# Layer 0 of a two-layer triangle-multiplication kernel: every projection unit as 64-row tiles, and two masks in four on VectorE

## The chip, the cores and the metric

The kernel runs on one NeuronCore of a Trainium2 chip. The metric is the device time of one launch, in microseconds. The kernel before has a median of 1039.27 us over three runs (1038.81 to 1039.66). The engines are named as in the profile: PE is TensorE (PEld its weight loads), DVE is VectorE, ACT is ScalarE, POOL is GpSimd, SP is SyncE, whose queue issues the DMAs.

## The reference, cut to what matters

The input is x[1, 256, 256, 64] in float32. There are two layers, each added to x after a group norm. Layer 0, the one that the change touches, is

```
zn = ln(gn(x))                                  # 256 x 256 tokens of 64 channels
a  = mask * sigmoid(zn @ w_ag + b_ag) * (zn @ w_ap + b_ap)
b  = mask * sigmoid(zn @ w_bg + b_bg) * (zn @ w_bp + b_bp)
p  = einsum('bikc,bjkc->bijc', a, b)
x  = x + (ln(p) @ w_z + b_z) * sigmoid(zn @ w_g + b_g)
```

Layer 1 is like it, without a mask, with whole-tensor norms in place of the layer norms, and with einsum('bitc,bjtc->bijc').

## The kernel before, in words

**Layout.** A row of 256 tokens is held as 128 partitions = 2 parities (q) x 64 channels, by 128 columns. Four rows are a group (64 groups), eight rows (PR) are a unit (NP = 32 units). The transposed, normalised x stays in SBUF as two float16 halves (hi and lo), and so do the weights. A product of x and w is hi*hi + hi*lo + lo*hi, so three matmuls.

**Chunks.** The 64 channels of a and b are made in NQ = 4 chunks of 16. For each chunk `chunk(q)` on the PE first projects the 32 units, and then does 16 einsum steps (one for each channel, four float32 matmuls of 256 columns in two halves). The two parts alternate: projections of chunk 0, einsum of chunk 0, projections of chunk 1, and so on. The PE projects units 2 to 31 of chunk q, then units 0 and 1 of the next chunk ahead, and then waits for all masks of the chunk (`msk_done`, `msk_done_v`) before the einsum.

**A unit in layer 0.** It passes four engines:

- PE, `project(q, n)`: 8 rows x 3 passes into the PSUM banks 2s and 2s+1, s = n % 4. The stationary operand is the x of one row (128 columns), the moving one the weights. What form the matmuls have is decided by `split_rows(layer, n)`, that is by SPLIT_ROWS. An even unit of layer 0 is split: two matmuls with 64 rows and 64 moving columns for each row and pass, one for each half of the array (`half_rows`), 48 in all. An odd unit is whole: one matmul with 128 rows and 128 moving columns, 24 in all. The halves of an even unit lie with their parities exchanged (`crossed(g)`), which the bank index `t ^ crossed(g)` undoes. A unit n of 4 or more waits for the product of unit n-4 (`prod_done`), which frees its banks.
- ACT, L971: one sigmoid of 128x512 from PSUM into the tile sig[u % 4]. It waits for the unit's matmuls and for the mask of the unit four before it, which reads the same tile (`masks_before`).
- DVE, L1397: the product of the linear part (PSUM) and the gate (SBUF), in place in sig.
- the mask, L377 (`mask_tile`): sig times the mask, both in SBUF, into ab. Of four masks the DVE does the one whose index u % 4 is in MASKS_V = (1,), and POOL does the other three. The DVE's own mask of unit u-1 stands in its queue right behind the product of unit u (`products(q, n8)`); POOL's waits for the product of its own unit.

**Order.** All orders are written by hand as each engine's instruction stream with semaphores. The DVE does the 32 products (with its masks among them), then for each of the 16 channels two additions of sums (L1416, L1419). ACT does the sigmoids, among them those of units 0 and 1 of the next chunk, and then two PSUM reads a channel (L1007, L1011). POOL has nothing but its masks in this stage. SP stores p in pairs of channels while the einsum runs. After chunk 3 the PE does the first four output gates (`project_gate`) in place of the next chunk's units.

**Layer 1** has units of both forms too (SPLIT_ROWS[1]), with two more matmuls a unit for a bias; units 2 and 3 of each eight are both split and follow one another. There the halves are never crossed.

Two lines show the widths that the form of a unit sets:

```
last = mm(PS[:, bank, r * QW:(r + 1) * QW], x[half_rows, :], w[half_rows, ...QW])   # split: QW = 64
last = mm(PS[:, 2 * s + r // GR, ...ROW], x, w[:, q * ROW:(q + 1) * ROW], ...)      # whole: ROW = 128
```

Of the kernel before, what the change touches and what calls it, by code (L numbers as in the profile page):

```python
# [76 lines left out]
E_Z = E_G + ROW  # L77
E_N = E_Z + ROW
UB = 8
SPLIT_ROWS = ((0, 2, 4, 6), (0, 2, 3, 5, 7))  # L80
EPS = 1e-5
Z_SCALE = 2.0 ** 8
W_TOP = 2.0 ** 13
# [13 lines left out]
def build(nc, x, mask, w0, w1, bias0, bias1, vecs, consts, norm_consts, spread, ones3, out):  # L97
# [16 lines left out]
    with ctx:  # L114
# [34 lines left out]
        def split_rows(layer, u):  # L149

            return u % UB in SPLIT_ROWS[layer]

# [184 lines left out]

        def crossed(g):

            return int(g // 2 % 2 in SPLIT_ROWS[0])  # L340

        assert all(split_rows(0, u) == crossed(2 * u) for u in range(UB))

        def group_rows(g):

# [7 lines left out]

            return tile.rearrange("p (b n) -> p b n", b=2)

        MASKS_V = (1,)
        MASKS_P = 4 - len(MASKS_V)

        def masks_before(n4, u):

            v = u % 4
            fours = n4 + u // 4
            if v in MASKS_V:
                return msk_done_v, fours * len(MASKS_V) + MASKS_V.index(v) + 1
            return msk_done, fours * MASKS_P + sum(w not in MASKS_V for w in range(v + 1))

# [155 lines left out]
        def _(pe):  # L522
# [98 lines left out]
            for step in range(max(NG + SUMS_LAG, spreads[-1][0] + 1)):  # L621
                if step < NG and step % 2 == 0:
                    n = step
                    reached(pe, sq_ready, n - 1)
                    for m in range(n, n + 2):
                        for q in range(2):
                            rows, to = (slice(h * CH, (h + 1) * CH) for h in (q, q ^ crossed(group_of(m))))
                            last = mm(cs_bank(m)[to, :], cs[rows, rows], group_rows(group_of(m))[rows, :])
                    last.then_inc(mm1_done, 2)
                n = step - SUMS_LAG  # L630
                if 0 <= n < NG:
                    square_sums(round_of[n], n - FIRST[round_of[n]])
                if step == 3:

                    small([(PS[:, 7, P:2 * P], ones, diag),
                           (PS[:, 7, 2 * P:2 * P + 1], out_sq, ones[:, 0:1])])
                for at_step, t, u in spreads:
                    if at_step == step:
                        spread_rstd(t, u)

            for layer in range(2):
# [19 lines left out]
                def project(q, n, bias=True):  # L661
# [12 lines left out]
                    for r in range(PR):  # L674
                        g, at_r = 2 * n + r // GR, r % GR
                        hi, lo = (half(g, i)[:, at_r * P:(at_r + 1) * P] for i in range(2))
                        for i, (x, w) in enumerate(((hi, w_hi), (hi, w_lo), (lo, w_hi))):
                            if split_rows(layer, n):
                                ends = r == 0 and i == 0, r == PR - 1 and i == 2
                                for t in range(2):  # L680
                                    half_rows = slice(t * CH, (t + 1) * CH)
                                    bank = 2 * s + (t ^ crossed(g) if layer == 0 else t)
                                    last = mm(PS[:, bank, r * QW:(r + 1) * QW], x[half_rows, :],
                                              w[half_rows, (2 * q + t) * QW:(2 * q + t + 1) * QW],
                                              ends[0] and not begun, ends[1] and (layer == 0 or begun))
                            else:
                                ends = at_r == 0 and i == 0, at_r == GR - 1 and i == 2
                                last = mm(PS[:, 2 * s + r // GR, at_r * ROW:(at_r + 1) * ROW], x,
                                          w[:, q * ROW:(q + 1) * ROW],
                                          ends[0] and not begun, ends[1] and (layer == 0 or begun))  # L690
# [39 lines left out]
                def chunk(q):  # L730
# [16 lines left out]
                    if layer == 0:  # L747
                        pe.wait_ge(msk_done, (q + 1) * (NP // 4 * MASKS_P))
                        pe.wait_ge(msk_done_v, (q + 1) * (NP // 4 * len(MASKS_V)))
                    else:  # L750
# [349 lines left out]
        def _(pool):  # L1100
# [13 lines left out]
            with pool.Fori(0, NQ) as q:  # L1114
                with pool.Fori(0, NP // 4) as n4:
                    for u in range(4):
                        if u not in MASKS_V:
                            pool.wait_ge(prod_done[0], q * NP + (n4 * 4 + (u + 1)))
# [557 lines left out]
```

## Time and profile before

| | |
|---|---|
| median of the runs | 1039.27 us (1038.81 to 1039.66) |
| the profiled execution | 1042.83 us, 3.56 us (0.34%) above that median |
| its span, first to last instruction | 1040.9 us |
| mean granted TensorE clock | 0.953 of full |
| busy over the span | PE 89%, DVE 73%, ACT 65%, POOL 46% |
| layer 0, projections of the four chunks | from 197, 266, 332 and 398 us |
| layer 0, einsums of the four chunks | from 236, 302, 367 and 433 us |

Times in the views are microseconds from the start of the span, unless marked ns. A row of a timeline merges instructions of one kind that follow each other, so that "x3" over 1.88 us is three of them, overlapping at their ends as their records do. The ends of matmuls are modelled; their starts are not, so the pace of the PE is read from counts in a stretch.

### The profile page before, as it was taken

What the parts mean: (1) busy time and instruction counts of PE and PEld (TensorE: products, weight loads), DVE (VectorE), ACT (ScalarE), POOL (GpSimd) and SP (SyncE); (2) the same over time, 40 slices, a digit from 0 to 9 for tenths busy, and PEclk for the clock granted to TensorE, in tenths of its full rate; (3) what the DMA queues carried; (4) which work ended last, traced back from release to release, by engine and by line L of the source; (5) the groups of instructions that cost most, each with busy time, mean ns of one, the idle gap of its engine ahead of it and who ended that gap; (6) DMA issues with size and microseconds to landing.
All of it is one profiled execution on the core that took longest, in us unless ns stands there. A gap on an engine that the chain in (4) does not pass through costs nothing.

```text
span 1040.9 us, 40845 instructions
## 1 busy us (share of the span) xinstructions
PE 927.0 (89%) x16740; PEld 743.7 (71%) x16740; DVE 763.9 (73%) x1276; ACT 673.4 (65%) x1104; POOL 476.6 (46%) x416
## 2 busy tenths in 40 slices
PE   5857877799999999978999996899999999869997
PEld 5732334698888988867898995678878788635554
DVE  5765898776868768688999998755646556458886
ACT  4659883566656666565777774575857758447775
POOL 0002667780752916506877882580936719200000
PEclk9879997799999999999999997899999999889999
DMA  9900000003113021179998940006032050389995
GB/s 333 377 23 2 2 2 2 3 4 121 45 43 122 4 106 60 49 215 261 223 217 192 219 91 1 3 4 163 4 89 78 7 160 4 89 200 294 359 325 192
DMA packets 159905, 122.06 MB, mean 117 GB/s; under 512 B 70788, under 2 KB 136708, under 8 KB 157704
## 3 DMA queue, kind: packets, MB, share of 16 engines
q1 hardware_dynamic: 159752, 119.74, 40.2%
q8 instruction: 131, 2.15, 0.9%
q14 instruction: 22, 0.18, 0.1%
HBM read 69.38 MB, written 50.33 MB: 115 GB/s over the span
## 4 chain that ended last, share of the span: by engine, by line
PE 74%; DVE 8%; ACT 6%; DMA 4%; issue 3%; POOL 2%; SPq 1%; DVEq 0%; POOLq 0%; ACTq 0%
PE PS L524 64%; PE PS L826 3%; DMA AB<-x 3%; PE PS L841 3%; ACT XT_ALL L931 2%; PE PS L873 2%; ACT AB L936 2%; PE PS L538 1%; POOL AB L377 1%; DVE AB L1359 1%; DMA AB<-k_scratch 1%; DVE XT_ALL L1361 1%; DVE XT_ALL L1529 1%; ACT WK L971 1%; SPq L391 1%
## 5 line engine op out<-in xcount | busy, mean ns | idle before, releaser
L524 PE MATMUL PS<-EFF,XT_ALL 64*128 64x64 f16 (+1 forms) x11112 | 326.3, 199 | 8.3 <-POOL XT_ALL L1105 3.2
L524 PEld LDWEIGHTS PS<-EFF,XT_ALL 64*128 64x128 f16 (+1 forms) x11112 | 296.6, 97 | 50.7 <-issue 25.8
L524 PE MATMUL PS<-AB 64*128 64x128 bf16 (+2 forms) x2058 | 239.9, 287 | 28.2 <-DVE XT_ALL L1361 13.0
L524 PEld LDWEIGHTS PS<-AB 64*128 64x128 bf16 (+2 forms) x2058 | 200.2, 123 | 68.5 <-issue 22.1
L971 ACT ACTIVATE WK<-PS,T 128x512 f32<-128x512 f32 x256 | 174.4, 685 | 94.8 <-PE PS L524 83.4
L1169 POOL TENSOR_TENSOR AB<-WK,AB 128x512 f32 x128 | 145.1, 1165 | 111.0 <-ACT AB L981 110.2
L377 POOL TENSOR_TENSOR AB<-WK,MS 128x512 f32 x96 | 130.6, 1390 | 105.5 <-DVE WK L1397 105.4
L1105 POOL TENSOR_TENSOR XT_ALL<-AB,XT_ALL 128x512 f16<-128x512 f32 x60 | 71.1, 1188 | 125.4 <-DVE XT_ALL L1361 120.4
L1405 DVE TENSOR_TENSOR WK<-PS,WK 128x512 f32<-128x512 f32 x128 | 85.8, 687 | 31.8 <-ACT WK L971 31.6
L1397 DVE TENSOR_TENSOR WK<-PS,WK 128x512 f32<-128x512 f32 x128 | 86.7, 689 | 30.2 <-ACT WK L971 25.0
L1421 DVE BATCH_NORM_STATS2 REC<-WK 128x512 f32 x64 | 44.5, 695 | 59.6 <-ACT WK L1000 59.6
L1000 ACT ACTIVATE WK<-PS,T 128x512 f32<-128x512 f32 x64 | 44.0, 688 | 54.4 <-PE PS L524 54.4
L1007 ACT ACTIVATE WK<-PS 128x512 f32<-128x512 f32 x64 | 41.1, 643 | 46.8 <-PE PS L524 46.8
L524 PEld LDWEIGHTS PS<-EFF,WK 128*128 128x128 f32 x512 | 68.5, 194 | 1.7
L524 PE MATMUL PS<-EFF,WK 128*128 128x128 f32 x512 | 68.0, 276 | 0.0
L1024 ACT ACTIVATE WK<-PS,T 128x512 f32<-128x512 f32 x64 | 46.4, 775 | 32.7 <-PE PS L524 32.7
L1416 DVE TENSOR_TENSOR S<-S,WK 128x512 f32<-128x512 f32 x64 | 44.6, 697 | 31.1 <-ACT WK L1007 30.3
L1067 ACT ACTIVATE WK<-PS 128x512 f32<-128x512 f32 x64 | 38.2, 597 | 44.2 <-PE PS L841 44.2
L1140 POOL TENSOR_TENSOR WK<-AB,S 128x256 f32<-128x256 f32 x64 | 50.5, 790 | 35.3 <-DVE S L1449 34.8
L981 ACT ACTIVATE AB<-WK 128x512 f32 (+1 forms) x96 | 60.0, 625 | 6.9 <-DVE WK L1405 6.9
L931 ACT ACTIVATE XT_ALL<-PS,T,CF 128x512 f32<-128x512 f32 x64 | 49.9, 780 | 18.1 <-PE PS L524 18.0
L1474 DVE SCALAR_TENSOR_TENSOR WK<-PS,T,WK 128x512 f32<-128x512 f32 x64 | 45.1, 746 | 21.8 <-PE PS L524 21.8
(199 smaller groups left out, 1435.5 us busy)
## 6 DMA issues: line engine op xcount, KB each, us to landing
AB<-x SPq DMA_DIRECT2D x64, 512.0 KB, 6.9
p_scratch<-WK SPq DMA_DIRECT2D x32, 512.0 KB, 2.6
k_scratch<-WK SPq DMA_DIRECT2D x128, 128.0 KB, 1.9
AB<-k_scratch SPq DMA_DIRECT2D x32, 512.0 KB, 11.1
out<-AB SPq DMA_DIRECT2D x16, 1024.0 KB, 7.6
AB<-p_scratch SPq DMA_DIRECT2D x29, 512.0 KB, 8.0
AB<-p_scratch SPq DMA_DIRECT2D x2, 640.0 KB, 5.7
AB<-spread SPq DMA_DIRECT2D x1, 896.0 KB, 7.4
```

The source lines that it names most:

```text
L377: return eng.tensor_tensor(ab[:, :, :, ds(n4 * (4 * PR) + u * PR, PR)], sig[:, u], rows.unsqueeze(2).to_broadcast([P, 2, 2 * CHUNK, PR]), ...
L524: return nc.tensor.matmul(dst, lhsT, rhs, start=start, stop=stop)
L931: nc.scalar.activation(group_rows(group_of(n)), cs_bank(n), ACT.Identity, bias=T[:, 15:16], scale=CF[:, C_NE0:C_NE0 + 1]).then_inc(zc_done, 1)
L971: nc.scalar.activation(tile, unit(layer, u)[:, :, 0:2 * CHUNK, :], ACT.Sigmoid, scale=T[:, 22:23] if layer == 0 else T[:, 28:29]).then_inc ...
L981: nc.scalar.activation(ab_rows(ab_hi, n8, u), sig1[:, u % UB], ACT.Copy).then_inc(abhi_done, 1)
L1024: nc.scalar.activation(gate1[:, k % 4], PS[:, k % 2, :], ACT.Sigmoid, bias=T[:, 32:33], scale=T[:, 28:29]).then_inc(gate1_ready, 1)
L1105: nc.gpsimd.tensor_tensor(lo, zn[:, n % 8], hi, ALU.subtract).then_inc(lo_done, 1)
L1140: nc.gpsimd.tensor_tensor(dst[:, 1], src[:, 1, :, u * GR:(u + 1) * GR, :], rs.to_broadcast([P, CH // 2, GR, 2]), ALU.mult).then_inc(pn_don ...
L1169: nc.gpsimd.tensor_tensor(ab_rows(ab_lo, n8, u), sig1[:, u], ab_rows(ab_hi, n8, u), ALU.subtract).then_inc(ablo_done, 1)
L1397: V.tensor_tensor(gate, lin, gate, ALU.mult).then_inc(prod_done[0], 1)
L1405: V.tensor_tensor(gate, lin, gate, ALU.mult).then_inc(prod_done[1], 1)
L1474: V.scalar_tensor_tensor(gate1[:, k % 4], PS[:, 4 + k % 2, :], col(34), gate1[:, k % 4], ALU.add, ALU.mult).then_inc(y1_done, 1)
```

## The change

SPLIT_ROWS[0] names all eight units, so the odd units of layer 0 take the split form as well; `crossed` keeps its values (1 for the groups of even units, 0 for those of odd ones), now written without SPLIT_ROWS. MASKS_V becomes (0, 2): the DVE multiplies the masks of the even units, each right behind the product of the odd unit that follows, and POOL those of the odd ones. The waits, `masks_before` and the counts MASKS_P follow from MASKS_V.

```
-SPLIT_ROWS = ((0, 2, 4, 6), (0, 2, 3, 5, 7))
+SPLIT_ROWS = (tuple(range(8)), (0, 2, 3, 5, 7))
...
         def crossed(g):
 
-            return int(g // 2 % 2 in SPLIT_ROWS[0])
-
-        assert all(split_rows(0, u) == crossed(2 * u) for u in range(UB))
+            return int(g // 2 % 2 == 0)
+
+        assert all(split_rows(0, u) or not crossed(2 * u) for u in range(UB))
...
-        MASKS_V = (1,)
+        MASKS_V = (0, 2)
         MASKS_P = 4 - len(MASKS_V)
```

## Rows read from the trace of the kernel before

**Rows 1.** The page, part 4: the chain that ended last, by engine.

```profile
PE 74%; DVE 8%; ACT 6%; DMA 4%; issue 3%; POOL 2%; SPq 1%; DVEq 0%; POOLq 0%; ACTq 0%
```

**Rows 2.** That chain in order of time, layer 0: start us, us, what.

```profile
196.97 34.84 PE PS L524 x1044
...
236.33 27.91 PE PS L524 x128
267.09 30.18 PE PS L524 x984
...
300.50 1.27 POOL AB L377
301.81 27.91 PE PS L524 x128
...
367.42 27.91 PE PS L524 x128
...
433.04 27.92 PE PS L524 x128
```

**Rows 3.** Groups by form, 267.1 to 297.3: count | busy us, mean ns | idle before.

```profile
L377 POOL TENSOR_TENSOR AB<-WK,MS 128x512 f32 x22 | 30.0, 1397 | 32.2 <-DVE WK L1397 32.2
...
L1397 DVE TENSOR_TENSOR WK<-PS,WK 128x512 f32<-128x512 f32 x29 | 19.6, 688 | 5.7 <-ACT WK L971 4.9
L971 ACT ACTIVATE WK<-PS,T 128x512 f32<-128x512 f32 x28 | 19.1, 687 | 12.7 <-PE PS L524 9.8 <-DVE MS L1419 1.3 <-POOL AB L377 0.8
...
L377 DVE TENSOR_TENSOR AB<-WK,MS 128x512 f32 x7 | 6.5, 934 | 0.0
```

**Rows 4.** Stretches: PE, PEld, DVE, ACT, POOL busy (x count); PEclk, DMA share, GB/s.

```profile
267.00:297.00 30.00, 29.91 (x978) 27.90 (x980) 24.61 (x36) 18.54 (x28) 28.49 (x21) 1.00 0.03 7
...
276.10:276.90 0.80, 0.80 (x50) 0.76 (x48) 0.80 (x2) 0.61 (x1) 0.80 (x2) 1.00 0.00 0
276.90:278.35 1.45, 1.45 (x30) 1.34 (x24) 1.45 (x3) 0.76 (x2) 1.45 (x1) 1.00 0.04 11
690.40:692.30 1.90, 1.90 (x102) 1.57 (x98) 1.00 (x3) 1.87 (x4) 1.70 (x3) 1.00 0.04 9
...
77.00:90.00 13.00, 8.22 (x120) 2.71 (x120) 6.53 (x22) 13.00 (x23) 0.00 (x0) 1.00 0.01 2
...
197.00:198.24 1.24, 1.24 (x48) 1.24 (x48) 1.11 (x2) 0.00 (x0) 0.22 (x1) 0.50 0.06 13
...
202.40:206.00 3.60, 3.60 (x100) 3.42 (x96) 2.02 (x4) 2.06 (x3) 2.55 (x2) 1.00 0.02 5
```

**Rows 5.** Timeline of PE in layer 1, two split units in a row.

```profile
690.47 0.86 PE L524 MATMUL PS<-EFF,XT_ALL 64*128 64x64 f16 x48
691.17 0.38 PE L524 MATMUL PS<-BIASR,ONES 64*128 64x512 bf16 x2
691.39 0.86 PE L524 MATMUL PS<-EFF,XT_ALL 64*128 64x64 f16 x48
```

**Rows 6.** Timeline of DVE where chunk 1's products begin.

```profile
266.35 1.88 DVE L1397 TENSOR_TENSOR WK<-PS,WK 128x512 f32<-128x512 f32 x3
268.15 0.90 DVE L377 TENSOR_TENSOR AB<-WK,MS 128x512 f32 x1
268.97 2.78 DVE L1397 TENSOR_TENSOR WK<-PS,WK 128x512 f32<-128x512 f32 x4
271.67 1.54 DVE L377 TENSOR_TENSOR AB<-WK,MS 128x512 f32 x1
```

**Rows 7.** Timeline of DVE, ACT and POOL about masks: a free pair, and POOL's first.

```profile
284.58 0.69 DVE L1397 TENSOR_TENSOR WK<-PS,WK 128x512 f32<-128x512 f32 x1 [0.20 <-ACT WK L971]
285.19 0.68 DVE L377 TENSOR_TENSOR AB<-WK,MS 128x512 f32 x1
...
285.46 1.55 POOL L377 TENSOR_TENSOR AB<-WK,MS 128x512 f32 x1 [0.32 <-DVE WK L1397]
...
267.22 1.28 POOL L377 TENSOR_TENSOR AB<-WK,MS 128x512 f32 x1 [30.94 <-DVE WK L1397]
```

**Rows 8.** Timeline of DVE: the first products of chunks 0, 2 and 3.

```profile
197.13 1.29 DVE L1397 TENSOR_TENSOR WK<-PS,WK 128x512 f32<-128x512 f32 x2 [1.23 <-POOL XT_ALL L1105]
...
331.96 0.69 DVE L1397 TENSOR_TENSOR WK<-PS,WK 128x512 f32<-128x512 f32 x1
...
397.58 0.69 DVE L1397 TENSOR_TENSOR WK<-PS,WK 128x512 f32<-128x512 f32 x1
```

## The prediction

> **What bounds the kernel now.** I read the chain that ended last first, then what lies in it in layer 0, then the groups and short stretches of one projection stage. The PE holds 74% of the chain [rows 1]. In layer 0 the chain runs through the projections on the PE (34.84 and 30.18 us in one piece), jumps at their end to the sigmoid, product and mask of the last units, and goes on with the einsum [rows 2]. So a stage of projections is set by the PE's pace plus a tail through ACT, DVE and POOL, and the einsum (27.91 us each) does not change here.
>
> The PE's pace comes from two short stretches: a split unit takes 0.80 us (48 weight loads), a whole one 1.45 us (24) [rows 4]. Four units take 2 x 2.25 = 4.51 us, 1.13 us each. The other engines in the same stage [rows 3]: the DVE has 4 products of 0.688 and one mask, ACT 4 sigmoids of 0.687, both with idle time; POOL has three masks of 1.397, 4.19 us of the 4.51, and is busy 28.5 us of 30 [rows 4]. POOL is the next bound, close behind the PE. Sped up alone, the PE would only hand over to POOL; this is why the two edits must be costed together.
>
> I count a stage from its first product to the einsum that follows. Chunk 1: 266.35 to 301.81, 35.46 us; chunk 2: 331.96 to 367.42; chunk 3: 397.58 to 433.04, all 35.46 us [rows 2, 6, 8]. Chunk 0: 197.13 to 236.33, 39.20 us [rows 2, 8]; it begins at half the clock.
>
> **PE, part by part.** 64 odd units (16 a chunk) go from 24 to 48 matmuls and weight loads each. Layer 1 shows split units in a row: the first matmul at 690.47, the next unit's bias at 691.17 [rows 5], so 0.70 us for 48 matmuls. Between unlike units layer 0 pays about 0.1 us more. After the change a unit costs the PE 0.70 us (at most 0.80) against 1.13. The Trainium skill says, on its page TensorEngine Tiling (Array Packing), section Key Properties, that changing the tiling mode drains the engine; the trace agrees (0.80 beside a whole unit, 0.70 among split ones). ACT needs 0.69 us a unit.
>
> **The masks.** The DVE takes one more in four, POOL one fewer. What matters is how the two engines' masks get in each other's way. A DVE mask costs 0.68 us alone [rows 7], but 0.90 or 1.54 us when POOL is inside one of its own [rows 6], and POOL's mask of 1.28 us [rows 7] takes 1.55 when it starts 0.27 us behind a DVE mask [rows 7]. So these two run one after the other: 1.55 + 0.27 = 1.82 us for the pair, of which the DVE's holds the first 0.54. Products, which read PSUM, stay at 0.688 with POOL busy all the time. The Trainium skill has this on its page SBUF — State Buffer, section SBUF: two separate sides: a DVE operation with two SBUF inputs and a GpSimd operation lock each other out, and whichever starts first keeps the port for the whole instruction.
>
> Who starts first after the change follows from the order of the code. The DVE issues product 2k, product 2k+1, mask 2k. POOL's mask 2k+1 waits for product 2k+1 and starts 0.27 us after the DVE's mask began, as in [rows 7] (product ends at 285.27, POOL starts 0.19 later). It ends at 1.82. The DVE's next mask is due after one mask and two products. The records of back-to-back DVE operations overlap: three products in 1.88 us, and the mask begins 1.80 after the first of them [rows 6], so the pitch is 0.60 us. Its next mask is due at 3 x 0.60 = 1.80, when POOL is just ending; of a wait of 0.02 us nothing is lost for long, since it cannot grow. The DVE stays in front, two units take 1.80 us, 0.90 each.
>
> The other loops stand this: the PE needs 0.70 and ACT 0.69 a unit. ACT's sigmoid 2k+5 waits for POOL's mask 2k+1. Counted from product 2k, that mask ends at 1.20 + 1.82 = 3.02, the sigmoid at about 3.75, and product 2k+5 is due at 4.20: 0.4 us of slack. The even units have more. **So the DVE becomes the bound, at 0.90 us in place of 1.13.**
>
> **The stage.** From the first product to the last: 31 products and 15 masks at 0.60 = 27.60 us. The tail: product 0.68, start of POOL's mask 0.19, that mask behind the DVE's last 1.55, start of the einsum 0.05 (300.50 + 1.27 to 301.81, [rows 2]) = 2.47. Sum 30.07 us against 35.46: 5.39 less. The PE's two units ahead and the gate projections of chunk 3 are done before that, because they wait for products 28 and 29 only; their cover is 2 us. The first product of a stage doesn't move: the sums of the einsum before it release it. Three stages: **-16.2 us**.
>
> Chunk 0: at half clock a split unit takes 24 x 0.0533 = 1.28 us (48 matmuls in 1.24, clock 0.50) [rows 4]. Units 2 to 5 start at 196.97 + 1.28 each and end at 202.1; the clock was full from 202.4 [rows 4], and I leave it there. Product 5 comes at 203.0, mask 4 at 203.6, product 6 at 204.2. From there the DVE bounds: 25 products and 12 masks up to product 31, 22.2 us, and the tail 2.47: the einsum starts at 228.9, **-7.4 us**.
>
> All that follows only shifts: einsum, stores, output stage and layer 1 are untouched. Sum -23.6 us: the profiled execution would go from 1042.83 to about 1019.2, and as that one stood 3.56 above the median, the median goes to **1015.7 us**.
>
> Bounds of what the trace doesn't show. A loop of products at the DVE's own pace past an end of its hardware loop (four a stage): between nothing and 0.3 us each, the gap of the records there being covered by waits now; 0 to 5 us in all, and I take 0, since the queue's work runs during the 0.69 us of an operation. The clock's rise in chunk 0 could come some us earlier or later: -1 to +2 us. A tail without the lock: -1 us. Own range 1012.5 to 1022.
>
> **The rivals.**
> - *The DVE pays full records.* If in a long row products and masks cost 0.69 and 0.68 and not 0.60, a stage takes 31 x 0.69 + 15 x 0.68 + 2.47 = 34.06 us, 1.4 less than now; chunk 0 ends 4.1 earlier: -8.3 us, 1031.0. Against it stand the four products in 2.78 us of [rows 6]. Chance 0.15. An odd unit whose halves don't run side by side would cost the PE 1.4 us and give nearly the same time; the units of [rows 5] are uncrossed as well, and take 0.70. Chance 0.02.
> - *The port turns against it (slower).* If POOL gets ahead of the DVE in the pair (its mask under way when the DVE's is issued), each DVE mask costs up to 1.54 us, pitch 1.46: 31 x 0.60 + 15 x 1.46 + 2.2 = 42.7 us a stage, 7.2 more: +29 us, 1068. It decides from the point at which the mean DVE mask has a record of 1.06 us, as then the stage is 35.46 again. Today's mean is 0.934 [rows 3], near enough to be taken seriously. Against it: today POOL is backlogged with three masks of four, afterwards it has 1.28 + 0.54 us of work in each 1.80, and is released only behind the DVE. Chance 0.06.
> - *Instruction supply (slower).* The PE issues 1958 instructions in 30 us now, 65 a us [rows 4]; the new stage wants 96 in 0.90 us, 107. Were 65 all that can be kept up, a unit would take 1.47 us, a stage some 11 us more: about 1084. Against it: 200 in 1.90 us in layer 1 [rows 4], 105 a us, though only for two units. The Trainium skill speaks of about 20 cycles of the sequencer for each instruction on its page Runtime: NRT & Kernel Launch, section Instruction fetch mechanics, and of 1.2 GHz for the sequencer on TensorE: Matmul & The Clock Gate, Part 1; as an estimate from the two, 96 would take 1.6 us. The trace has 96 in 0.70 us, so I hold the burst against the rule. Chance 0.04.
> - *The clock.* The PE will idle 0.2 us in each 0.90. If the granted clock fell to 0.50, a unit would take 1.28 us, 4 to 5 us more a stage than now and more in the einsum: about 1060. Against it: 77 to 90 us, PE busy 8.22 of 13, clock 1.00 [rows 4]. Chance 0.02.
> - *No change* (gain and loss in balance, within 0.2% or 2 us, about what a measurement of this kernel tells from none). Chance 0.03.
>
> **How the numbers follow.** Forecast 0.68, smaller gain 0.17, slower 0.12, none 0.03; so faster 0.85, same 0.03, slower 0.12. The range reaches from the low end of the forecast over the smaller gain, 1012.5 to 1032, and leaves out what is above.
>
> **What would show it.** In the profile after: einsum starts some 7 us earlier in chunk 0 and 5.4 more with each following; in the projection stages PE idle before matmuls, released by DVE L1397; DVE idle near zero, its masks' mean between 0.68 and 0.75; POOL's masks near 1.55, each just behind a DVE mask; POOL busy 85%. A DVE mask mean above 1 us, PE gaps with no releaser, or a clock below 1.00 from 210 us on would each name the rival that won.

## The result and the profile after

The change is slower. Median 1060.92 us over four runs (1060.05 to 1064.94) against 1039.47 for the kernel before beside it: ratio 1.0218, 95% interval 1.0205 to 1.0232, so about 21 us more where 24 less were forecast. The profiled execution took 1061.16 us, span 1059.3.

The page of the kernel after: busy time, the queue that brings instructions, the chain by engine, and two groups, the projections' matmuls of both layers and POOL's masks.

```profile
PE 885.1 (84%) x18276; PEld 705.5 (67%) x18276; DVE 770.9 (73%) x1308; ACT 669.4 (63%) x1104; POOL 443.7 (42%) x384
...
q8 instruction: 143, 2.34, 1.0%
...
PE 70%; issue 8%; DVE 8%; ACT 7%; DMA 4%; POOL 2%; SPq 1%; DVEq 0%; POOLq 0%; ACTq 0%
...
L524 PE MATMUL PS<-EFF,XT_ALL 64*128 64x64 f16 (+1 forms) x12648 | 284.9, 196 | 68.1 <-issue 56.7
...
L377 POOL TENSOR_TENSOR AB<-WK,MS 128x512 f32 x64 | 98.5, 1539 | 161.3 <-DVE WK L1397 161.3
```

The same group and the same queue on the page of the kernel before:

```profile
q8 instruction: 131, 2.15, 0.9%
...
L524 PE MATMUL PS<-EFF,XT_ALL 64*128 64x64 f16 (+1 forms) x11112 | 326.3, 199 | 8.3 <-POOL XT_ALL L1105 3.2
```

The PE is busy for less (it was 927.0 us), and its share of the chain fell from 74% [rows 1] to 70%. What came in its place is "issue", 3% before and 8% now: time in which the engine waited for nothing that the profile shows. The PE stands idle 68.1 us before the projections' matmuls (8.3 before), 56.7 of them under that name.

The chain in order of time shows the pattern in the projections of chunk 1 (start us, us, what):

```profile
270.26 1.19 PE PS L524 x70
271.46 0.85 issue
272.31 2.04 PE PS L524 x128
274.35 1.69 issue
276.04 2.04 PE PS L524 x128
278.08 1.41 issue
279.49 2.04 PE PS L524 x128
281.54 1.41 issue
282.95 2.04 PE PS L524 x128
```

Each run of matmuls has exactly 128, and a pause follows. 128 matmuls and their 128 weight loads are 256 instructions, and a unit is 96, so the pauses come in the middle of units, where no semaphore is waited for. The same count stands in the queue for instructions: the change adds 3072 PE instructions (1536 matmuls and as many weight loads), and 12 packets (131 before, 143 now), one for each 256. In all nine kernels of this document the packets of q8 are the PE's instructions divided by 256 and rounded up (36552 / 256 = 142.8 here). So the PE gets its program in blocks of 256 instructions, and a block starts 3.45 to 4.01 us after the one before, however fast it is executed. The last full block of the stage is followed by one that starts at 304.77; from 272.31 to there are nine blocks, 3.61 us each, 71 instructions a us. Over the 34 blocks of this kind in all four stages the mean is 3.68 us.

The packets can be seen one by one. The queues over 10 us, in 40 slices of 0.25 us from 272.31, hold three packets and nothing else:

```profile
GB/s 0 0 0 0 66 0 0 0 0 0 0 0 0 0 0 0 0 0 0 66 0 0 0 0 0 0 0 0 0 0 0 0 0 66 0 0 0 0 0 0
...
q8 instruction: 3, 0.05, 2.0%
```

Their records start at 273.36, 277.07 and 280.59 us and last 1.12, 0.98 and 1.12 us. Each starts 1.03 to 1.10 us after a block did (272.31, 276.04, 279.49), and the next block starts 1.24 to 1.56 us after its end. The same holds in the 34 blocks: the packet starts 1.03 to 1.67 us into the block, lasts 0.88 to 1.43 us, and the next block starts 1.21 to 1.56 us after its end. Where a block took 3.45 us, the first two terms add up to 1.96 to 2.21 us; where it took 4.00, to 2.47 to 2.60. So the fetches follow one another, each begun only after the PE has started on a new block, and the time of that round sets the pace; the transfer itself is less than half of it.

Two stretches and a pause between them (PE, PEld, DVE, ACT, POOL busy; PEclk, DMA share, GB/s):

```profile
276.04:278.20 2.16, 2.04 (x128) 1.93 (x128) 1.29 (x3) 1.26 (x2) 1.64 (x2) 1.00 0.03 8
278.20:279.40 1.20, 0.00 (x0) 0.00 (x0) 1.20 (x3) 0.05 (x1) 0.23 (x1) 1.00 0.00 0
290.60:294.10 3.50, 3.30 (x128) 3.15 (x128) 1.92 (x3) 1.96 (x3) 1.09 (x2) 0.57 0.02 5
...
235.60:265.60 30.00, 29.97 (x132) 26.57 (x134) 20.40 (x30) 16.69 (x30) 0.00 (x0) 0.93 0.31 124
```

Inside a block the PE is at the forecast pace: 128 matmuls have records of 2.04 us together, and their starts lie 14.6 ns apart, 0.70 us for 48. In the pause it does nothing at all, and no DMA moves a byte. The third row shows a block at a lower granted clock, after such pauses; it took 3.30 us, and as the next block started 3.73 us after it, 1.28 us behind the end of its packet, the slow clock cost nothing there. In the fourth the lower clock reaches into the einsum of chunk 0, which took 29.99 us in place of 27.91.

Where the time went, in the two profiled executions, from a stage's first product to its einsum. The first products after are these (timeline of the DVE), and the einsums begin as the chain has them:

```profile
191.63 0.69 DVE L1397 TENSOR_TENSOR WK<-PS,WK 128x512 f32<-128x512 f32 x1 [2.34 <-POOL XT_ALL L1105]
...
267.73 0.68 DVE L1397 TENSOR_TENSOR WK<-PS,WK 128x512 f32<-128x512 f32 x1
...
338.71 0.69 DVE L1397 TENSOR_TENSOR WK<-PS,WK 128x512 f32<-128x512 f32 x1
...
410.15 0.69 DVE L1397 TENSOR_TENSOR WK<-PS,WK 128x512 f32<-128x512 f32 x1
```

```profile
235.63 29.99 PE PS L524 x128
...
308.55 27.92 PE PS L524 x128
...
379.99 27.91 PE PS L524 x128
...
451.27 27.91 PE PS L524 x128
```

Chunk 0: 44.00 us (39.20 before); chunks 1 to 3: 40.82, 41.28 and 41.12 (35.46 before). Together 21.6 us more, and 2.1 for the einsum at the lower clock. Against that the first product came 5.5 us earlier than in the profiled execution of before (191.63 against 197.13, [rows 8]). That is no gain of the change: in the traces of the experiments below it comes at 190.92 to 194.05 us, with whole odd units or without, and the profiled execution of before was the late one. Sum 18.2 us; the two executions differ by 18.3.

### The profile page after: what moved, and what is told of

It reads as the page before. It is cut to its first block, busy times and chain, and to the rows that moved or that the text cites. A ratio compares the mean times of both kernels' runs of the same rounds, so it can differ in the third digit from the quotient of the medians.

```text
span 1059.3 us, 43885 instructions
## 1 busy us (share of the span) xinstructions
PE 885.1 (84%) x18276; PEld 705.5 (67%) x18276; DVE 770.9 (73%) x1308; ACT 669.4 (63%) x1104; POOL 443.7 (42%) x384
## 4 chain that ended last, share of the span: by engine, by line
PE 70%; issue 8%; DVE 8%; ACT 7%; DMA 4%; POOL 2%; SPq 1%; DVEq 0%; POOLq 0%; ACTq 0%
PE PS L524 60%; PE PS L826 3%; DMA AB<-x 3%; PE PS L841 3%; ACT XT_ALL L931 2%; PE PS L873 2%; ACT AB L936 2%; PE PS L538 1%; POOL XT_ALL L1105 1%; DMA AB<-k_scratch 1%; DVE XT_ALL L1361 1%; DVE XT_ALL L1529 1%; DVE WK L1397 1%; POOL AB L377 1%; ACT WK L971 1%
## 5 line engine op out<-in xcount | busy, mean ns | idle before, releaser
L524 PE MATMUL PS<-EFF,XT_ALL 64*128 64x64 f16 (+1 forms) x12648 | 284.9, 196 | 68.1 <-issue 56.7
L524 PEld LDWEIGHTS PS<-EFF,XT_ALL 64*128 64x128 f16 (+1 forms) x12648 | 259.8, 97 | 106.4 <-issue 87.5
L971 ACT ACTIVATE WK<-PS,T 128x512 f32<-128x512 f32 x256 | 171.8, 685 | 118.3 <-PE PS L524 104.0
L377 POOL TENSOR_TENSOR AB<-WK,MS 128x512 f32 x64 | 98.5, 1539 | 161.3 <-DVE WK L1397 161.3
L1397 DVE TENSOR_TENSOR WK<-PS,WK 128x512 f32<-128x512 f32 x128 | 84.3, 686 | 45.1 <-ACT WK L971 42.4
L1405 DVE TENSOR_TENSOR WK<-PS,WK 128x512 f32<-128x512 f32 x128 | 85.8, 686 | 32.6 <-ACT WK L971 32.1
L1000 ACT ACTIVATE WK<-PS,T 128x512 f32<-128x512 f32 x64 | 44.0, 687 | 53.3 <-PE PS L524 53.3
L1024 ACT ACTIVATE WK<-PS,T 128x512 f32<-128x512 f32 x64 | 46.3, 773 | 32.6 <-PE PS L524 32.6
```

The source lines that it names most:

```text
L377: return eng.tensor_tensor(ab[:, :, :, ds(n4 * (4 * PR) + u * PR, PR)], sig[:, u], rows.unsqueeze(2).to_broadcast([P, 2, 2 * CHUNK, PR]), ...
L524: return nc.tensor.matmul(dst, lhsT, rhs, start=start, stop=stop)
L971: nc.scalar.activation(tile, unit(layer, u)[:, :, 0:2 * CHUNK, :], ACT.Sigmoid, scale=T[:, 22:23] if layer == 0 else T[:, 28:29]).then_inc ...
L1024: nc.scalar.activation(gate1[:, k % 4], PS[:, k % 2, :], ACT.Sigmoid, bias=T[:, 32:33], scale=T[:, 28:29]).then_inc(gate1_ready, 1)
L1397: V.tensor_tensor(gate, lin, gate, ALU.mult).then_inc(prod_done[0], 1)
L1405: V.tensor_tensor(gate, lin, gate, ALU.mult).then_inc(prod_done[1], 1)
```

## The experiments

**Theory.** The PE's instructions arrive in blocks of 256, one each 3.45 us at the fastest and 3.6 in the mean (of chunk 1). A stage is bound by whichever is longer, the work or its instructions. **Rivals.** The second mask on the DVE; the 64-row form itself; the chain of ACT, DVE and POOL.

**The masks alone** (e1_masks_only), the changed kernel with

```
-SPLIT_ROWS = (tuple(range(8)), (0, 2, 3, 5, 7))
+SPLIT_ROWS = ((0, 2, 4, 6), (0, 2, 3, 5, 7))
```

> The masks alone: the odd units of layer 0 stay whole, MASKS_V is (0, 2). Theory (the PE's instructions come in blocks of 128 matmuls and 128 weight loads, one block each 3.6 us, so about 14 ns an instruction): a pair of units has 144 instructions, 2.0 us, below the 2.25 us that its matmuls take, so the PE's pace stays 1.13 us a unit and the time 1037 to 1041 us. Rival (the second mask on the DVE costs the time, by waits for the port shared with GpSimd): a stage gets longer by the 5 us that it did in the changed kernel, 1055 us or more, with DVE masks above 1 us.

1038.21 us, ratio 0.9989 (0.9977 to 1.0). Groups by form from 272 to 296:

```profile
L377 POOL TENSOR_TENSOR AB<-WK,MS 128x512 f32 x11 | 17.0, 1544 | 7.8 <-DVE WK L1397 7.8
...
L377 DVE TENSOR_TENSOR AB<-WK,MS 128x512 f32 x10 | 6.8, 682 | 0.0
```

The DVE's masks run free, at 682 ns (934 in [rows 3]), and POOL's are 1544, each behind one of the DVE's. The masks are not the cause.

**The matmuls alone** (e2_split_only), the changed kernel with

```
-        MASKS_V = (0, 2)
+        MASKS_V = (1,)
```

> The matmuls alone: all units of layer 0 split, MASKS_V stays (1,). Theory (supply of instructions): 96 a unit at 14 ns is 1.35 us, above the 1.05 us that GpSimd needs for three masks in four, so the loss is whole: 1057 to 1063 us, the PE stopping after each 128 matmuls. Rival (the masks): near 1039 or below.

1058.94 us, ratio 1.0183 (1.0155 to 1.0211): nearly the whole loss, in the same pattern (timeline of the PE):

```profile
272.58 2.04 PE L524 MATMUL PS<-EFF,XT_ALL 64*128 64x64 f16 x128 [1.41 <-issue]
276.04 2.04 PE L524 MATMUL PS<-EFF,XT_ALL 64*128 64x64 f16 x128 [1.41 <-issue]
279.76 2.04 PE L524 MATMUL PS<-EFF,XT_ALL 64*128 64x64 f16 x128 [1.69 <-issue]
```

**As many instructions, no 64-row tile more** (e4_halved_whole), the kernel before with the odd units' matmuls cut in two along the moving columns:

```
-                                last = mm(PS[:, 2 * s + r // GR, at_r * ROW:(at_r + 1) * ROW], x,
-                                          w[:, q * ROW:(q + 1) * ROW],
-                                          ends[0] and not begun, ends[1] and (layer == 0 or begun))
+                                parts = 2 if layer == 0 else 1
+                                N = ROW // parts
+                                for h in range(parts):
+                                    last = mm(PS[:, 2 * s + r // GR, at_r * ROW + h * N:at_r * ROW + (h + 1) * N], x,
+                                              w[:, q * ROW + h * N:q * ROW + (h + 1) * N],
+                                              ends[0] and h == 0 and not begun,
+                                              ends[1] and h == parts - 1 and (layer == 0 or begun))
```

> The kernel before, with each 128-column matmul of an odd unit of layer 0 made as two of 64 columns with all 128 rows: as many matmuls (48 a unit) as the split form, and no 64-row tiles more. Theory (number of instructions): 96 a unit at 14 ns is 1.35 us against 1.13 before, so it is as slow as the changed kernel, 1057 to 1065 us, with pauses after each 128 matmuls. Rival (something in the 64-row form, as two halves that get in each other's way): the columns are as before, 48 x 0.029 = 1.40 us, so 1039 to 1043 us.

1064.40 us, ratio 1.0248 (1.0217 to 1.0279). Timeline of the PE:

```profile
266.85 1.57 PE L524 MATMUL PS<-EFF,XT_ALL 128*128 128x64 f16 x48 [0.40 <-ACT WK L1015]
...
272.67 3.43 PE L524 MATMUL PS<-EFF,XT_ALL 128*128 128x64 f16 x128 [0.24 <-issue]
276.68 2.96 PE L524 MATMUL PS<-EFF,XT_ALL 64*128 64x64 f16 x128 [0.58 <-issue]
280.42 3.77 PE L524 MATMUL PS<-EFF,XT_ALL 64*128 64x64 f16 x133 [0.78 <-issue]
```

The first line is one odd unit at its own pace, hardly more than the 1.45 us of a whole one; with the 0.80 us of an even unit the matmuls of a pair would take what they took before. Yet a pair has 192 instructions, three quarters of a block, and the blocks start 3.5 to 4.0 us apart here too (3.72 in the mean of the stages), with shorter pauses as the matmuls fill more of that time. The number of instructions alone makes the loss; nothing is left for the 64-row form.

**Fewer instructions, all units split** (e5_two_passes), the changed kernel with one pass left out in layer 0:

```
                         for i, (x, w) in enumerate(((hi, w_hi), (hi, w_lo), (lo, w_hi))):
+                            if layer == 0 and i == 1:
+                                continue
```

> The changed kernel without the pass hi * w_lo in the projections of layer 0 (the output is less exact by that part): 64 instructions a unit in place of 96. Theory (supply): 64 x 14 ns = 0.90 us, equal to the DVE's 0.90 us a unit, so a stage takes 30 to 32 us from first product to einsum, and the time is 1016 to 1026 us; it would show that the rest of the prediction's schedule holds once instructions are there. Rival (the schedule of DVE, GpSimd and ACT is what takes 1.3 us a unit): stages stay near 40 us, the time above 1050.

1018.84 us, ratio 0.9807 (0.9789 to 0.9824); the profiled execution took 1012.93, the lowest of its runs. The stage of chunk 1, from the timeline of the DVE and the chain in order of time:

```profile
251.06 0.68 DVE L1399 TENSOR_TENSOR WK<-PS,WK 128x512 f32<-128x512 f32 x1
```

```profile
252.26 0.68 DVE AB L377
...
254.05 0.68 DVE AB L377
...
279.51 1.53 POOL AB L377
281.08 29.34 PE PS L524 x128
```

30.02 us from first product to einsum; the prediction had 30.07. The other three stages took 30.03 to 30.13. The DVE's masks follow one another at 1.80 us, as it had them too, and the PE waits for the DVE (from 251.1 to 280 us: PE idle 8.3 us, all behind L1399, and none under "issue"). A pair of units has 128 instructions, so 71 a us is a rate that the supply does keep up. Once the PE's program arrives in time, the schedule of the DVE, ACT and POOL is as forecast; this kernel has a third less work for the PE, so the PE's 0.70 us a unit is shown by the blocks of the kernel after and not by this one. (The einsum behind the stage took 29.34 us in place of 27.91, and that of chunk 2 30.95, with a mean granted clock of 0.95 and 0.90; the other two kept 27.9. Two of four stages with an idling PE were followed by a lower clock, at a cost of 4.5 us.)

**How much can be split** (e3_five_split, e7_six_split): between the 72 instructions a unit of before and the 96 of after.

```
-SPLIT_ROWS = (tuple(range(8)), (0, 2, 3, 5, 7))
+SPLIT_ROWS = ((0, 2, 3, 4, 6), (0, 2, 3, 5, 7))        # e3_five_split
+SPLIT_ROWS = ((0, 2, 3, 4, 6, 7), (0, 2, 3, 5, 7))     # e7_six_split
```

> Units 0, 2, 3, 4 and 6 of each eight split, 1, 5 and 7 whole, masks as in the changed kernel: 624 instructions for eight units, 78 a unit. Theory (a block of 256 instructions each 3.45 us at the fastest, 3.6 in the mean): 8.4 to 8.8 us for eight units, 1.05 to 1.10 a unit, while the matmuls alone would take 1.02; against 1.13 before this is 0.5 to 2 us less a stage: 1029 to 1037 us. Rival (only the matmuls count): 1.02 a unit, 1024 to 1026 us. Rival (any unit more in the split form costs, whatever the supply): above 1041.

> Units 0, 2, 3, 4, 6 and 7 of each eight split, 1 and 5 whole: 672 instructions for eight units, 84 a unit. Theory (supply of a block each 3.45 to 3.6 us): 1.13 to 1.18 us a unit against 1.13 before, so 1037 to 1046 us, slower than with five split units although the matmuls take less (0.92 a unit); the pauses after 128 matmuls are back. Rival (only the matmuls and the DVE count): near 1014 to 1018 us.

Five of eight: 1036.34 us, ratio 0.9979 (0.9967 to 0.9991), faster than the kernel before by 0.2%. Six of eight: 1040.72, ratio 1.0013 (0.9999 to 1.0028), no gain though its matmuls are shorter. Timeline of the PE with five split, then with six:

```profile
270.81 7.52 PE L524 MATMUL PS<-EFF,XT_ALL 64*128 64x64 f16 x256 [1.42 <-issue]
278.54 3.25 PE L524 MATMUL PS<-EFF,XT_ALL 64*128 64x64 f16 x128 [0.21 <-issue]
282.27 6.67 PE L524 MATMUL PS<-EFF,XT_ALL 64*128 64x64 f16 x256 [0.48 <-issue]
```

```profile
272.46 3.25 PE L524 MATMUL PS<-EFF,XT_ALL 64*128 64x64 f16 x128 [1.69 <-issue]
276.46 3.25 PE L524 MATMUL PS<-EFF,XT_ALL 64*128 64x64 f16 x128 [0.76 <-issue]
279.92 3.25 PE L524 MATMUL PS<-EFF,XT_ALL 64*128 64x64 f16 x128 [0.21 <-issue]
```

With five some blocks last as long as the next one takes to come (the merged x256); with six each block in these rows starts behind a pause.

**The masks where instructions don't bind** (e8_two_passes_masks1): e5_two_passes with `MASKS_V = (1,)`.

> All units split and without the pass hi * w_lo in the projections of layer 0 (the output is less exact by that part), but with MASKS_V = (1,): three masks in four on GpSimd. Theory: with the supply out of the way GpSimd bounds a stage, 3 masks of 1.28 us and 0.54 of waiting for the DVE's one in four units, 1.10 us a unit, so the time is 1031 to 1038 us against 1018.8 with MASKS_V = (0, 2); the second mask on the DVE would then be worth 12 to 18 us. Rival (the place of the masks makes no difference): within 3 us of 1018.8.

1036.12 us, ratio 0.9971 (0.9959 to 0.9982), 17 us behind e5_two_passes. Groups by form from 272 to 296:

```profile
L377 POOL TENSOR_TENSOR AB<-WK,MS 128x512 f32 x15 | 20.8, 1424 | 0.0
L973 ACT ACTIVATE WK<-PS,T 128x512 f32<-128x512 f32 x19 | 12.6, 687 | 7.1 <-POOL AB L377 7.1
L377 DVE TENSOR_TENSOR AB<-WK,MS 128x512 f32 x5 | 8.3, 1654 | 0.0
```

POOL is never idle, and each DVE mask takes 1654 ns because POOL is always inside one of its own. This is the mechanism of the rival in which the port turns against the DVE; it belongs to three masks in four on POOL, not to the change.

All nine kernels; each of the seven experiments came out inside the range that its theory had stated:

| kernel | PE instructions a unit, mean | masks on DVE | median us |
|---|---|---|---|
| before | 72 | 1 in 4 | 1039.47 |
| e1_masks_only | 72 | 2 in 4 | 1038.21 |
| e3_five_split | 78 | 2 in 4 | 1036.34 |
| e7_six_split | 84 | 2 in 4 | 1040.72 |
| e2_split_only | 96 | 1 in 4 | 1058.94 |
| e4_halved_whole | 96 | 1 in 4 | 1064.40 |
| after | 96 | 2 in 4 | 1060.92 |
| e8_two_passes_masks1 | 64 | 1 in 4 | 1036.12 |
| e5_two_passes | 64 | 2 in 4 | 1018.84 |

From 78 instructions a unit upwards the times grow with them, whatever form the matmuls have; at 64 it is the masks that decide. The packets beside the pauses show what the PE waits for. What makes up the 1.0 to 1.7 us before a packet starts and the 1.2 to 1.6 after its end is not shown, and nothing was tried that could shorten them.

## Why the prediction was wrong

- **What bounded the kernel before:** right, and incomplete. The PE's matmuls set the pace, at 2.25 us for two units. Not seen: their 144 instructions, at 14.1 ns each, need 2.03 us. POOL, which the prediction took for the next bound, was 7% away (4.19 of 4.51 us), and the second edit moved it; the supply was 10% away, and nothing moved it. A gain of 20% a unit was counted on.
- **The step that failed: "After the change a unit costs the PE 0.70 us (at most 0.80)".** Inside a block that is so. But 96 instructions take 96/256 of 3.61 us, 1.35 us, to arrive, above the 1.13 of before and the DVE's 0.90. The stages of chunks 1 to 3 got 5.4 to 5.8 us longer in place of 5.4 shorter, that of chunk 0 4.8 longer in place of 7.4 shorter.
- **How it failed.** The mechanism stood among the rivals, with a chance of 0.04 and its right sign (PE gaps with no releaser), set aside by the 200 instructions in 1.90 us of [rows 4]. That burst is less than one block. It shows how fast instructions run once they are there, and nothing of how fast they come. For a rate that must hold for 30 us, the row to weigh was the long one, and 267 to 297 us held 65 a us [rows 4]. Its price, 1084 us, took those 65 for the limit; those were the pace of the matmuls, and in chunk 1 the supply gave 71, which makes 96/71 = 1.35 us a unit and, over 31 units, some 7 us more a stage than before; 5.4 to 5.8 were measured, as a stage begins with instructions already there (262 matmuls, 48 + 48 + 96 + 70, before the first pause in chunk 1).
- **The Trainium skill's rule**, weighed and set aside. Its page Runtime: NRT & Kernel Launch, section Instruction fetch mechanics, has about 20 cycles for each instruction, which the prediction's estimate made 1.6 us a unit: the right side, but not the mechanism, as 256 run in 2.04 us inside a block, 8 ns each. The same section calls the fetch in blocks of 256 hidden. The size agrees with the packets here; "hidden" does not, with 56.7 us of issue.
- **Masks, port, tail and DVE's pitch:** right, each. DVE masks 0.68 us, POOL's 1.54, the tail 2.47 us (306.08 to 308.55 after chunk 1), and with the supply out of the way 30.02 us a stage against 30.07. The second mask on the DVE is worth 17 us there, and about 1, at the edge of what can be measured, where the PE is the bound.
- **The clock:** held to be nearly no risk on the row from 77 to 90 us. The traces after do not bear that out. The clock fell at times in the stages (0.57 in one block), and cost 2.1 us in one einsum; in e5_two_passes, which keeps the forecast schedule but whose PE idles more than the forecast had it, the lower clock cost 4.5 us in two. This term stood at nothing in the sum; it is small beside the 45 us by which the forecast missed.

## What to carry to other kernels

Before cutting matmuls into more and shorter ones, count instructions as a resource of their own: weight loads and matmuls together, over the whole length of the stage, against the highest rate that any stretch of many blocks has held. A burst shorter than a block of instructions is no evidence for a rate. Where both bounds are near, mix the forms so that they balance, here five split units of eight, worth 0.2%; the sign of the other bound is "issue" idle time after equal counts of instructions.

## What the runs showed of the hardware that was not expected

- The PE executes 256 instructions (128 matmuls of 64x64 and their loads) in 2.04 us and then stops until 3.45 to 4.01 us after the block's start, in both kernels in which all units are split and all three passes kept (after, e2_split_only).
- The packet with instructions starts 1.03 to 1.67 us after the PE has begun a block, lasts 0.88 to 1.43 us, and the next block begins 1.21 to 1.56 us after its end (34 blocks of the kernel after). The sum of these three, and not the bandwidth, is what 256 instructions cost.
- The stock is small: after an einsum the first pause comes after 262 matmuls, 524 instructions.
- The time from block to block doesn't depend on the form of the matmuls: with 128x64 ones a block takes 3.43 us, and the next starts only 0.58 us later.
- A unit's cost in instructions can outweigh its columns: six split units of eight have the shorter matmuls, and take 4.4 us more than five.
